# Projection pairs in other PSUM banks, the key activations in one run, and the last diagonal copies on VectorE

## The reference

```python
mixed = hidden_states @ W_qkv.T                  # 2048 channels
y = conv(mixed, 4 taps, causal, depthwise)
mixed = silu(y)                                  # q, k: 8 heads of 64; v: 16 heads of 64
g, beta = decay and gate of each of 16 heads
def step(Sst, inp):                              # token by token
    q_t, k_t, v_t, g_t, b_t = inp
    Sst = Sst * jnp.exp(g_t)[..., None, None]
    kv = jnp.einsum('bhkv,bhk->bhv', Sst, k_t)
    delta = (v_t - kv) * b_t[..., None]
    Sst = Sst + k_t[..., None] * delta[..., None, :]
    o = jnp.einsum('bhkv,bhk->bhv', Sst, q_t)
```

## Time and profile before

| | |
|---|---|
| median of three executions | 1478.57 us |
| the profiled execution, by the same clock | 1480.8 us |
| its span from first to last instruction | 1478.9 us |
| mean granted TensorE clock | 0.927 of full |
| busy: TensorE / its weight loads | 1301.2 / 916.3 us |
| busy: VectorE / ScalarE / GpSimd | 908.9 / 701.8 / 313.6 us |
| share of the chain that ended last | PE 54%, DVE 28%, ACT 11%, issue 4%, POOL 2%, DMA 1% |

### The profile page before, as it was taken

How to read it: one execution, slowest core, us unless ns; L and a number is a source line. 1 busy time by engine, 2 the same in 40 slices (tenths; PEclk the granted TensorE clock), 3 DMA queues, 4 the chain that set the end, 5 groups by cost and what they waited for, 6 DMA issues and landing times.

```text
span 1478.9 us, 27509 instructions
## 1 busy us (share of the span) xinstructions
PE 1301.2 (88%) x11326; PEld 916.3 (62%) x11326; DVE 908.9 (61%) x2349; ACT 701.8 (47%) x1354; POOL 313.6 (21%) x234
## 2 busy tenths in 40 slices
PE   5778898898989899898988979998998989989898
PEld 3455756676666657566774546765666657666566
DVE  6887979899897989876446133542346333453321
ACT  3746474665648465564421435235452344524442
POOL 5141523525162352615110010000100000000100
PEclk9979899898989989897997589999999999999999
DMA  3000000000000000010400000000000000000000
GB/s 121 11 2 5 2 12 1 2 12 2 12 2 12 2 2 8 2 33 9 157 5 8 1 1 0 8 1 2 8 0 8 1 2 8 1 1 1 1 8 8
DMA packets 15068, 17.72 MB, mean 12 GB/s; under 512 B 2567, under 2 KB 13216, under 8 KB 14560
## 3 DMA queue, kind: packets, MB, share of 16 engines
q1 hardware_dynamic: 12768, 14.09, 2.8%
q0 software_dynamic: 576, 1.76, 0.4%
q10 hardware_dynamic: 1600, 0.12, 0.1%
HBM read 13.87 MB, written 2.10 MB: 11 GB/s over the span
## 4 chain that ended last, share of the span: by engine, by line
PE 54%; DVE 28%; ACT 11%; issue 4%; POOL 2%; DMA 1%; ACTq 0%; DVEq 0%; POOLq 0%
PE ps L1597 8%; PE ps L1607 8%; PE ps L1395 6%; DVE arena L1961 5%; DVE arena L1964 4%; PE ps L1147 3%; PE ps L1230 3%; DVE arena L2238 2%; ACT arena L1023 2%; PE ps L1702 2%; PE ps L1666 2%; PE ps L1301 2%; ACT arena L695 2%; ACT arena L719 2%; PE ps L1130 1%
## 5 line engine op out<-in xcount | busy, mean ns | idle before, releaser
L1876 DVE SCALAR_TENSOR_TENSOR arena<-ps,conv_w,arena 128x255 f32<-128x255 f32 (+2 forms) x384 | 163.5, 476 | 19.0 <-ACT arena L686 14.5
L985 ACT ACTIVATE arena<-ps 128x512 f32<-128x512 f32 x144 | 85.3, 597 | 179.4 <-PE ps L1597 179.3
L543 POOL TENSOR_TENSOR rstd<-var_eps,half_power 128x2 f32<-128x2 f32 (+1 forms) x28 | 23.3, 834 | 613.2 <-DVE var_eps L1847 613.1
L1607 PEld LDWEIGHTS ps<-arena 128*128 128x128 f32 x1152 | 132.6, 192 | 24.8 <-issue 9.9
L1607 PE MATMUL ps<-arena 128*128 128x128 f32 x1152 | 136.9, 277 | 7.1 <-ACT arena L985 4.1
L1597 PE MATMUL ps<-arena 128*128 128x512 f32 x288 | 133.0, 607 | 0.0
L2209 DVE SCALAR_TENSOR_TENSOR arena<-ps,gates,arena 128x128 f32<-128x128 f32 x128 | 36.0, 343 | 114.6 <-PE ps L1607 114.3
L537 POOL TENSOR_SCALAR arena<-arena 32x1024 f32<-32x1024 f32 x32 | 88.5, 2765 | 53.5 <-DVE arena L1975 51.5
L1961 DVE TENSOR_TENSOR arena<-arena 128x30 f32<-128x30 f32 (+14 forms) x240 | 95.2, 397 | 7.3
L2275 DVE TENSOR_REDUCE arena<-ps 128x8 f32<-128x2048 f32 (+1 forms) x24 | 54.9, 2293 | 62.2 <-PE ps L1666 62.2
L1964 DVE TENSOR_TENSOR arena<-arena 128x30 f32<-128x30 f32 (+14 forms) x240 | 83.8, 349 | 8.3
(11 more groups left out here) (249 smaller groups left out, 2897.6 us busy)
## 6 DMA issues: line engine op xcount, KB each, us to landing
arena<-in_routed_up SPq DMA_DIRECT2D x1, 2048.0 KB, 9.7
arena<-in_routed_down SPq DMA_DIRECT2D x1, 2048.0 KB, 14.2
x_ln<-in_x SPq DMA_DIRECT2D x8, 128.0 KB, 2.6
arena<-in_w_mix SPq DMA_DIRECT2D x1, 1024.0 KB, 6.4
x_in<-in_x SPq DMA_DIRECT2D x8, 128.0 KB, 2.4
out_x<-x_res SPq DMA_DIRECT2D x8, 128.0 KB, 1.9
arena<-out_x SPq DMA_DIRECT2D x4, 256.0 KB, 2.8
out_x<-arena SPq DMA_DIRECT2D x4, 256.0 KB, 2.2
```

The lines of the kernel that those rows point to most:

```text
L985: act.activation(hid1[half][:, i, :], ps[:, banks[i], :], ACT.Gelu).then_inc(s["mgelu"], 1)
L1607: mm = pe.matmul(ps[:, bank, c * P:(c + 1) * P], hid1[half][:, i, c * P:(c + 1) * P], m_down[:, e, i, :], start=(i == 0), stop=(i == HT1 - 1))
L1876: ins = dve.scalar_tensor_tensor(conv_tile(f, m)[:, sh:SEQ], ps[:, PAIR_BANK[p], j * SEQ:(j + 1) * SEQ - sh], conv_w[:, m, TAPS - 1 - sh:T ...
```

## The change

Pair 5 moves from bank 4 to bank 1, so it no longer waits for pair 3 but for pair 1, and pair 7 (bank 4) waits for pair 3 and no longer for pair 5. On TensorE the projection of pair 5 goes ahead of the first decay sum; the second decay sum, whose bank 1 is now taken until pair 5 is convolved, moves from ahead of pair 6 to behind all merges, ahead of the seven unread matmuls and the first key products; the third goes from behind the second key products to ahead of them. On ScalarE the four `silu` of q and k stand in one run behind the seed of pair 5 (before, they stood one by one behind the seeds of pairs 6 and 7 and the merges), and the first decay matrix follows directly on the seed of pair 7. The four 32x128 copies of the last batch move from ScalarE to VectorE, between its last products and `residual`, under a semaphore of their own.

```diff
-PAIR_BANK = (0, 1, 3, 4, 2, 4, 2, 4)
+PAIR_BANK = (0, 1, 3, 4, 2, 1, 2, 4)
@@ ScalarE, diagonal_blocks
-                for lo, hi in ((0, NB),) if c == 0 else ((0, NB - 1), (NB - 1, NB)):
...
+                hi = NB if c == 0 else NB - 1
+                act.wait_ge(s["at_ready"], CH * NB * n + NB * c + hi)
...
@@ ScalarE, the loop
                 if has_f:
                     seed(f, 5)
+                    for p in range(QK_TILES):
+                        silu(f, p)
                 if has_n:
                     solved64(n, 1, 0)
+                if has_f:
+                    seed(f, 6)
+                if has_n:
                     merged64(n, 0, 0)
...
-                    seed(f, 6)
-                    silu(f, 0)
...
                     seed(f, 7)
-                    silu(f, 1)
+                    decay_matrix(f, 0)
                 if has_n:
                     merged64(n, 1, 0)
...
-                    silu(f, 2)
...
                     merged64(n, 1, 1)
...
-                    silu(f, 3)
-                    decay_matrix(f, 0)
                     decay_matrix(f, 1)
                     decay_matrix(f, 2)
@@ TensorE, project
                 if p >= 5:
-                    pe.wait_ge(s["conv_done"], NP * f + p - 1)
+                    pe.wait_ge(s["conv_done"], NP * f + (1, 4, 3)[p - 5] + 1)
@@ TensorE, decay_sums
                 if k < 2:
-                    pe.wait_ge(s["conv_done"], NP * n + k + 1)
+                    pe.wait_ge(s["conv_done"], NP * n + (0, 5)[k] + 1)
@@ TensorE, the loop
                 if has_f:
+                    project(f, 5, n, has_n)
                     decay_sums(f, 0)
-                    project(f, 5, n, has_n)
...
-                    decay_sums(f, 1)
                     project(f, 6, n, has_n)
...
+                    decay_sums(f, 1)
                     key_products(f, 0)
+                    decay_sums(f, 2)
                     key_products(f, 1)
-                    decay_sums(f, 2)
                     key_products(f, 2)
@@ VectorE
+            def last_diagonal_blocks(n):
+                dve.wait_ge(s["at_ready"], CH * NB * (n + 1))
+                after(dve, "b32_psum", 2 * n)
+                after(dve, "um_blocks", QUADS * n)
+                hs = slice(VH, 2 * VH)
+                for q in range(QUADS):
+                    r = slice(BLOCK * q, BLOCK * (q + 1))
+                    dve.tensor_copy(atc[r, hs, :]...[:, :, 2 * NB - 2:2 * NB, :],
+                                    at[r, hs, r]...[:, :, 2 * NB - 2:2 * NB, :]).then_inc(s["atl_ready"], 1)
@@ VectorE, steps_of_inverse
-                    dve.wait_ge(s["atc_ready"], 3 * QUADS * (n + 1))
+                    dve.wait_ge(s["atc_ready"], 2 * QUADS * (n + 1))
+                    dve.wait_ge(s["atl_ready"], QUADS * (n + 1))
@@ VectorE, the loop
                     products(me, n, 6)
                     products(me, n, 7)
+                    last_diagonal_blocks(n)
```

More of the change, by code:

```diff
@@ L321, in program @@
             "ktok_psum ktok_ready vtok_psum vtok_ready gm_ready sum_psum dm_ready kk_psum at_ready pt_ready "
-            "w1_in atc_ready t2_ready tt_ready uc_ready um_blocks a32_psum x32_ready b32_psum u32_ready tt32_ready a64_psum x64_ready "
+            "w1_in atc_ready atl_ready t2_ready tt_ready uc_ready um_blocks a32_psum x32_ready b32_psum u32_ready tt32_ready a64_psum x64_ready "
             "b64_psum u64_ready e_psum e_ready we_ready s_psum s_ready o_psum hz_ready hz_sq o_var o_rstd_ready "
@@ L713, in diagonal_blocks @@
                 after(act, "um_blocks", QUADS * n)
-                for lo, hi in ((0, NB),) if c == 0 else ((0, NB - 1), (NB - 1, NB)):
[L716 to L721, removed]
+                hi = NB if c == 0 else NB - 1
+                act.wait_ge(s["at_ready"], CH * NB * n + NB * c + hi)
+                for q in range(QUADS):
+                    r = slice(BLOCK * q, BLOCK * (q + 1))
+                    act.activation(atc[r, hs, :].rearrange("p (g y) n -> p g y n", g=2)[:, :, 0:2 * hi, :],
+                                   at[r, hs, r].rearrange("p (g y) n -> p g y n", g=2)[:, :, 0:2 * hi, :], ACT.Copy)\
+                        .then_inc(s["atc_ready"], 1)
             def solved32(n, c):
@@ L926, in _ @@
                     gate_of_tile(0, 0)
-                if has_f:
-                    seed(f, 6)
-                    silu(f, 0)
                 if has_n:
@@ L1949, in products @@
                 dve.tensor_tensor(d, qk[:, :, 0:1, :].to_broadcast([P, 2, 2, P]), d, ALU.mult).then_inc(s["pt_ready"], 1)
+            def last_diagonal_blocks(n):
[3 more added lines that the diff above has]
+                hs = slice(VH, 2 * VH)
+                for q in range(QUADS):
+                    r = slice(BLOCK * q, BLOCK * (q + 1))
+                    dve.tensor_copy(atc[r, hs, :].rearrange("p (g y) n -> p g y n", g=2)[:, :, 2 * NB - 2:2 * NB, :],
+                                    at[r, hs, r].rearrange("p (g y) n -> p g y n", g=2)[:, :, 2 * NB - 2:2 * NB, :])\
+                        .then_inc(s["atl_ready"], 1)
             def steps_of_inverse(me, n, first, last):
                 if first == 0:
-                    dve.wait_ge(s["atc_ready"], 3 * QUADS * (n + 1))
+                    dve.wait_ge(s["atc_ready"], 2 * QUADS * (n + 1))
+                    dve.wait_ge(s["atl_ready"], QUADS * (n + 1))
                     assert me.n == 0
```

## The result

Eight executions of each kernel on one chip: before 1474.70 us (median; 1471.13 to 1479.76), after 1465.67 us (1463.24 to 1471.61). The ratio is 0.9938 with a 95% interval of 0.9915 to 0.9960: 9 us faster, and 4.6 us above the forecast of 1461.1. So the change is worth 6 to 9 us, where the sum said 17.45.

What follows compares the result with a forecast made beforehand. No engine owns the end; VectorE runs nearly unbroken, with 38.1 us of waits for late seeds, last diagonal copies and first decay matrix. Gains of 13.3 + 1.3 + 2.85 = 17.45 us take 1478.57 to 1461.1, range 1455 to 1469.

Steps and rivals of the forecast that it cites:

- Pair 5, the silu run, the keys: Steady turns: first key products start 1.97 us earlier, taken as 1.9 in each of seven turns, 13.3 us in sum.
- VectorE's wait for the seed of pair 5 gone, that for pair 6 near 1.0: Sign of success at VectorE's convolutions in a steady turn: wait of 1.33 us gone, wait for pair 6 about 1.0.
- what it gave back: At the state products, 0.3 us of the copies' 0.65 lost again in a turn, leaving 0.35 in six turns.
- The last diagonal copies: Before the inverse's transpose: four VectorE copies of 0.25 us, transpose 0.65 earlier, 2.85 us kept in all.
- The first turn: Turn ahead of the inverting ones: no merge, VectorE's waits sum to 1.4 us, 1.3 taken as gain.
- Rival 4: Slower by the clock: TensorE stays at 1.2 GHz up to the keys, 5.6 us a turn, 1518 us; chance 0.05.
- the bound of 0.92: Whole kernel: the forecast would be wrong if TensorE's mean granted clock fell below 0.92.
- Rival 1: Half given back: two masks across the normalisation cost another 0.87 us a turn, or silu overruns; 1467 us; chance 0.14.
- Rival 2: Unread matmuls before the keys do not bind: 2.4 us a turn, copies keep 0.65; 1455.3 us; chance 0.06.
- Rival 3: Change does nothing: VectorE's wait only moves to the keys or state products; 1474 to 1479 us; chance 0.09.

Runs made afterwards that it cites:

- e1: Changed kernel with the first decay sum ahead of pair 5 again in the first turn alone; 1459.98 us, ratio 0.9884 to the kernel before.
- e9: Changed kernel without an edit, measured again in a later series; 1470.95 us, ratio 0.9961 to the kernel before.
- e5: Changed kernel with GpSimd's fifth mask of the first turn moved behind tile clearing, output-weight scaling and experts' weights; 1464.32 us, ratio 0.9930 to before.
- e4: Kernel before with pair 5 projected ahead of the first decay sum in the first turn alone; 1486.62 us, ratio 1.0058 to before.
- e3: Changed kernel with ScalarE's silu one by one, seeds and first decay matrix in their old places; 1465.94 us, ratio 0.9925 to before.
- e7: e1 with nine unread products in TensorE's idle time ahead of the first solve of turn 0; 1459.17 us, ratio 0.9894 to before.
- e8: e1 with silu one by one and the last diagonal copies back on ScalarE; 1470.00 us, ratio 0.9963 to before.
- e11: e10 with nine unread products ahead of the first solves of turns 0 and 6; 1460.50 us, ratio 0.9881 to before.
- e10: e1 run again, beside e9 on one chip; 1464.55 us, ratio 0.9919 to the kernel before.
- e12: e10 without any unread products in front of the first keys; 1460.99 us, ratio 0.9895 to the kernel before.

## Why the prediction was right, and where it was not

**The sign and the range held; the size did not.** The forecast said 17.45 us, measured were 9.0 and 6.0. At equal clock the change brings 1475.6 - 1462.9 = 12.7. So there are two losses: 4.7 us of work, and 0.0057 of mean clock, which by the slope of 0.81 is 4.6 us. 12.7 - 4.6 = 8.1, the difference of the mean spans; in time it is 0.4 less, since the part outside the span grew from 2.0 to 2.4 us where the forecast had kept it.

**Pair 5, the silu run, the keys: right.** "VectorE's wait for the seed of pair 5 gone, that for pair 6 near 1.0" is the row at 444.35 with 0.92; the wait for the keys was to be 0.4 and is 0.45. The step said 1.9 us a turn for these and 0.35 for the copies, 2.25; the profiled turns gave 2.47 in the steady ones and 2.26 over all seven. The seven turns between the transposes gave 15.8 us. The forecast has the same for them, 13.3 + 2.85 - 0.65 + 0.3 = 15.8, since 0.65 of its copies lies ahead of the first transpose and 0.3 of what it gave back behind the eighth. That the two agree to 0.1 is luck in part: the steady turns gave 0.2 more each than forecast, those without a wait for pair 6 up to 1.0 more, and turn 0 gave 0.8 less. That e1 has 16.4 at equal clock is the same statement by totals, but for the first turn.

**The last diagonal copies: right in size.** Taken as 0.25 us each, they took 0.24; taken as 2.85 us in all (2.5 between the first and the eighth transpose), they cost 3.0 (turns) to 3.6 (equal clock) when undone, though in the four steady turns 0.2 each where 0.35 was forecast.

**The first turn: the wrong sign.** The step "In the first turn there is no merge; its waits sum to 1.4, of which I take 1.3" is the one that failed. It read VectorE's waits in that turn and not who else waits for the first decay sum. GpSimd's fifth mask does, and in this turn alone it stands in front of some 15 us of clearing, scaling and DMA issues and of the first root. Instead of +1.3, and +0.65 for the copies ahead of the transpose, the turn gave -4.2 in after and -2.3 in e9, counted from the first convolution; e1 and e5, which take this wait away in two different queues, have the first transpose 5.9 and 6.7 us earlier (0.8 of e5's from earlier loads). e4 shows the same loss in the kernel before. The totals give back less, 3.7 us at equal clock: after's profiled first turn is on the late side (e9, the same kernel, has 62.20). With the wait taken away the turn gives +1.6 (42.01 to 40.37), near the forecast's 1.95, so it was the path over GpSimd that was missed and not the size of VectorE's waits. The miss of 6.1 us in after and 4.3 in e9 covers the 4.7 us of work. Behind it e1 has nothing to lose, its seven turns sum to 569.58, after's to 569.87.

**The clock: not priced.** Rival 4 asked for a fall in every steady turn, and that did not occur (the wait at the keys is 0.45, where the sum at full clock had 0.4). But the mean clock went from 0.9315 to 0.9258, above the bound of 0.92 that the prediction set as its alarm. Two places are seen, both at `gated`: in turns 0 and 6 its waits on TensorE are 1.92 us in before (L1994) and 7.68 in after. The rest of the 7.0 and 13.8 stands behind the loop, a wait of 5.09 in both and one of 1.02 that in before falls outside the first 720 us. In turn 6 it has no wait in before and 1.97 and 1.02 in after, where TensorE is at 0.50 from 637 to 640; e3 has the same there, so it isn't the silu run. It doesn't come every time either: e7 and e8 have the same idle 1.47 ahead of that solve and no fall. In turn 0 it waits 3.66 in after, 0.90 in before, and that turn gained only 1.24 of its 2.47. TensorE and the windows of after in turn 0:

```profile
132.83 6.47 PE L1288 MATMUL ps<-arena 128*128 128x64 f32 x32 [2.18 <-DVE arena L1949]
```
```profile
131.00:134.00 3.00, 1.17 (x9) 1.20 (x9) 2.80 (x8) 2.90 (x5) 0.00 (x0) 0.91 0.04 11
134.00:137.00 3.00, 3.00 (x16) 3.00 (x15) 2.79 (x7) 2.99 (x6) 0.00 (x0) 0.50 0.00 0
137.00:140.00 3.00, 3.00 (x14) 2.45 (x14) 2.76 (x8) 0.75 (x2) 1.33 (x2) 0.50 0.00 0
```

The solve takes 6.47 us in after, 3.79 in e7. In all eight profiled executions with the silu run and no filling, the turn from the second to the third transpose took 85.8 us or more; in e3 and e8, without the run, 82.60 and 82.90; in e7 and e11, with the filling, 81.79 and 82.22. e4, before's order without the run, had 84.24. But before, without the run, had 88.08. That the silu run as such brings the clock down is therefore not shown, and the greater part of the 0.0057 isn't traced to a place: most of it may lie in the first turn and behind the inverse, where single executions of one kernel differ as much (e1 and e10, the same kernel, have 0.931 and 0.921 in their profiled executions and spans of 1459.8 and 1466.3; 6.1 of these 6.5 us lie behind the eighth transpose, and up to the first one the clock was 0.94 and 0.88, where before had 0.94, after 0.87 and e9 0.92).

**The rivals.** Rival 1 priced two masks across the normalisation at another 0.87. In after the two do run beside it, and the pair takes 1.50, against 1.47 in the earlier trace rows with one. With the unread products gone they lie further over it, and it takes 1.69 (e12): the contention is there, as the rule of the Trainium skill that the prediction named (GPSIMD Engine Reference, Specifications) has it, but it goes with the time for which the two overlap (1.2 us in after, 1.6 in e12) rather than with the number of masks. This is a trend and not a law: e3's pair took 1.32 with 1.15 across it. The price of 0.87 was about right where both masks do lie across it: in the first turn of after the pair takes 2.24 (the row at 44.33), 0.77 more than with one. Rival 2 is out: the unread products do bind, by 0.45, and in the turn shown e12 could have had only 0.26 of it. Rival 3 is out by the 15.8 us.

## What to carry to other kernels

When two steps of a queue are exchanged, list every engine that waits for either, in the first and last turn of the loop too: what an engine has behind that wait may be 15 us of work that no steady turn shows. A wait filled with unread matmuls is worth looking for where TensorE idles ahead of a long run of small matmuls. And a total that scatters by 10 us with the granted clock can hide a part worth 4: compare turns in the trace, and spans at equal clock, before a part is called worth nothing, and ask whether the clock is the part's own doing before its worth at equal clock is counted as gained.

## What the runs showed of the hardware

- An idle stretch of 2.18 us on TensorE was followed by 1.2 GHz in nine of twelve profiled executions (e1, after and before among them), and by 2.4 GHz in three (e3, e4, e8); filled, it was followed by 2.4 GHz both times (e7, e11). 32 solve matmuls took 5.65 to 7.06 us behind the one and 3.76 to 3.79 behind the other.
- VectorE's copy of 32x128 in f32 took 0.24 us, ScalarE's 0.31 to 0.33.
- Two normalisations on VectorE (128x128 f32) took 0.60 us alone, 1.32 to 1.50 us with GpSimd's masks beside them for 1.0 to 1.2 us, 1.69 with 1.6 and 2.24 with 1.9.
- One kernel on one chip lay between 1463.4 and 1478.0 us (e9, twelve executions), its mean granted clock between 0.919 and 0.932.
